# Router logits taken from the first normalised tile, and routing two blocks behind instead of three

## The reference

```python
x = x + xattn(layernorm(x), ctx, Wq, bq, Wk, bk, Wv, bv, Wo, bo)
h = layernorm(x)
expert = argmax(h @ router_w.T + router_b)
y = relu(relu(h @ weights1[expert] + bias1[expert]) @ weights2[expert] + bias2[expert])
x = x + y
```

## Time and profile before

| | us |
|---|---|
| median of 3 runs | 1223.89 (1223.77 to 1226.08) |
| the profiled execution, its own time | 1223.15 |
| its span in the profile | 1221.3 |
| PE busy | 1097.5 (90%) |
| DVE busy | 925.0 (76%) |
| ACT busy | 858.5 (70%) |
| POOL busy | 847.3 (69%) |
| mean granted TensorE clock | 0.972 of full |

### The profile page before, as it was taken

One profiled execution on the slowest core, in us unless ns is written; L12 is line 12 of the kernel. 1 busy time (PEld: TensorE's weight loads), 2 busy tenths in 40 slices (PEclk: granted clock), 3 DMA queues, 4 the chain that ended last, 5 costly groups with the idle time before them and its releaser, 6 DMA issues.

```text
span 1221.3 us, 39225 instructions
## 1 busy us (share of the span) xinstructions
PE 1097.5 (90%) x15399; PEld 845.1 (69%) x15399; DVE 925.0 (76%) x2321; ACT 858.5 (70%) x2020; POOL 847.3 (69%) x1613
## 2 busy tenths in 40 slices
PE   5999999999999999999999999999998419998893
PEld 4777777777777777777777777777776319977772
DVE  4787888888888888888888888888877427866772
ACT  4777777777777777777777777777776306655551
POOL 4544777677777777777777777777764656777776
PEclk9999999999999999999999999999999859999997
DMA  7415222522222222222222222222110136676650
GB/s 243 147 56 121 71 72 71 142 80 76 76 73 79 82 83 75 80 71 72 72 78 74 72 71 72 71 72 72 59 41 29 52 132 205 198 215 205 205 161 17
DMA packets 91156, 120.40 MB, mean 99 GB/s; under 512 B 14096, under 2 KB 73883, under 8 KB 90781
## 3 DMA queue, kind: packets, MB, share of 16 engines
q1 hardware_dynamic: 77150, 84.04, 24.2%
q0 software_dynamic: 13824, 33.85, 7.7%
HBM read 60.61 MB, written 59.31 MB: 98 GB/s over the span
## 4 chain that ended last, share of the span: by engine, by line
PE 60%; DVE 20%; POOL 7%; DMA 5%; issue 4%; ACT 3%; SPq 1%; POOLq 0%; DVEq 0%; ACTq 0%
PE pB L832 10%; PE pA L774 9%; PE pB L824 8%; PE sc L782 7%; DVE mx L595 6%; PE sc L806 5%; POOL out L419 4%; PE sc L765 4%; PE sc L815 3%; ACT arena L468 3%; DVE nrm L621 3%; PE m L791 3%; PE sc L1000 3%; DMA out<-arena 2%; PE m L798 2%
## 5 line engine op out<-in xcount | busy, mean ns | idle before, releaser
L595 DVE TENSOR_REDUCE mx<-m 128x4 bf16<-128x512 f32 x512 | 322.6, 670 | 10.7 <-PE m L791 10.5
L468 ACT ACTIVATE arena<-sc 128x512 f32<-128x512 f32 x512 | 264.5, 603 | 47.5 <-PE sc L815 47.5
L419 POOL DMA_INDIRECT out<-arena x160 | 157.0, 981 | 60.9 <-issue 31.1
L615 DVE STREAM_TRANSPOSE tr<-pB 128x512 f32<-128x512 f32 x128 | 91.8, 717 | 106.3 <-PE pB L824 106.3
L806 PE MATMUL sc<-qk 32*128 32x256 f32 x2048 | 167.0, 397 | 0.5 <-DVE rbp L674 0.5
L824 PE MATMUL pB<-arena 128*32 128x128 f32 x4096 | 159.8, 276 | 1.5 <-issue 1.0
L386 POOL DMA_INDIRECT pages<-row,slot_i x128 | 130.4, 1019 | 40.0 <-issue 37.0
L832 PE MATMUL pB<-wo_s,aT 128*128 128x256 f32 x512 | 138.0, 392 | 8.7 <-DVE aT L626 8.7
L824 PEld LDWEIGHTS pB<-arena 128*32 128x32 f32 x4096 | 99.0, 109 | 44.6 <-issue 43.6
L774 PE MATMUL pA<-cHi,wqkv 128*128 128x512 f32 x252 | 119.0, 474 | 9.4 <-DVE wqkv L660 9.4
L774 PE MATMUL pA<-xnT,wqkv 128*128 128x512 f32 x372 | 124.7, 443 | 0.0
(11 more groups left out here) (141 smaller groups left out, 2714.9 us busy)
## 6 DMA issues: line engine op xcount, KB each, us to landing
arena<-pages SPq DMA_DIRECT2D x160, 130.0 KB
cT<-ctxT SPq DMA_DIRECT2D x64, 256.0 KB, 3.8
xs<-x_in SPq DMA_DIRECT2D x128, 128.0 KB, 3.3
pages<-empty SPq DMA_DIRECT2D x120, 130.0 KB, 3.1
pages<-empty SPq DMA_DIRECT2D x1, 5200.0 KB, 19.8
out<-arena POOLq DMA_INDIRECT x160
w2s<-w SPq DMA_DIRECT2D x1, 2080.0 KB
qk<-w SPq DMA_DIRECT2D x1, 2064.0 KB, 8.2
```

Source lines behind the costliest of these rows:

```text
L419: pool.indirect_dma_start(out_rows, bass.IndirectOffsetOnAxis(pr[:, r, COL_TOKEN:COL_TOKEN + 1].bitcast(U32), 0), pr[:, r, 0:D], None, bou ...
L468: act.activation(pt[:, u % 2, g].rearrange("p i k -> p (i k)"), sc[g][:, :], ACT.Exp).then_inc(S["exp_out"], 1)
L595: ins = dve.tensor_reduce(mx[:, 32 * g:32 * g + 4], mb[i][:, :].rearrange("p (h k) -> p h k", h=4), AX.X, ALU.max)
L615: dve.transpose(tr[:, :], pB[:, :]).then_inc(S["tr_out"], 1)
```

## The change

The centred router weights are multiplied into the output projection: `wo_s` and `bo_s` get 32 more columns, and so do `xs` and `row`. The part of the logits that comes from x itself is made from the first normalised tile: its transposed float32 copy `xnTf` goes through `logits` and `logits_transpose` a block ahead, in u=1, and VectorE (`x_logits`) multiplies with the deviation `sd1` and puts it into the 32 columns of `xs`. `residual` then adds both parts. `best` multiplies with the second norm's reciprocal deviation and adds the router's bias. `xn2`, its transposes and copies go. `xnT` and its low half are made from `xnTf` in SBUF. Routing runs one block earlier, `rstd2` once a block, `rstd1` a block earlier, `slot_sum`, `choose`, `scan` and some `stats1` stand ahead of `attended`. Setup makes the combined weights and biases. On SP the wait on `scattered` goes and the context loads move. The columns of `row` get another order.

```diff
-COL_TOKEN, COL_EXPERT, COL_MEAN, COL_RSTD = 256, 257, 258, 259
+COL_TOKEN, COL_EXPERT, COL_MEAN, COL_RSTD, X0 = 0, 1, 2, 3, 4
...
-            load_ctx(3, 0)
-            load_ctx(3, 1)
...
                     after(sp, "x2_out", 4, q, u)
-                    if u == 3 and q >= 2:
-                        after(sp, "scattered", 64, q - 2, 63)
                     if live(q + 4):
                         load_x(q + 4, u)
                     n = FIRST_PAGES + 4 * q + u
                     if n < PAGES:
                         sp.dma_start(page_view[:, n, :], empty[:, :]).then_inc(S[f"fill{q % 4}"], 16)
-                    if u == 3 and live(q + 4):
-                        load_ctx(q + 4, 0)
-                    if u == 0 and q >= 1 and live(q + 3):
-                        load_ctx(q + 3, 1)
+                    if u in (1, 2) and live(q + 3):
+                        load_ctx(q + 3, u - 1)
...
-                r, m, g = rs1[:, q % 2, :], nm1[:, q % 2, :], ag1[:, q % 2]
+                r, m, v, g = rs1[:, q % 2, :], nm1[:, q % 2, :], vr1[:, q % 2, :], ag1[:, q % 2]
                 after(pool, "agg1_out", 4, q, 3)
                 if q >= 2:
                     after(pool, "xn_out", 2, q - 2, 1)
-                pool.tensor_scalar(r, g[:, :, 1], EPS, None, ALU.add).then_inc(S["var1_out"], 1)
+                    after(pool, "lg_out", 1, q - 2, 0)
+                pool.tensor_scalar(v, g[:, :, 1], EPS, None, ALU.add).then_inc(S["var1_out"], 1)
                 after(pool, "var1_out", 1, q, 0)
-                pool.tensor_tensor(r, r, half[:, :], ALU.pow).then_inc(S["pow1_out"], 1)
+                pool.tensor_tensor(r, v, half[:, :], ALU.pow).then_inc(S["pow1_out"], 1)
                 after(pool, "pow1_out", 1, q, 0)
                 pool.tensor_tensor(m, g[:, :, 0], r, ALU.mult).then_inc(S["mr1_out"], 1)
+                pool.tensor_tensor(sd1[:, q % 2, :], v, r, ALU.mult).then_inc(S["std1_out"], 1)
                 after(pool, "mr1_out", 1, q, 0)
                 pool.tensor_scalar(m, m, -1.0, None, ALU.mult).then_inc(S["rstd1_out"], 1)
 
-            def rstd2(q, h):
-                r, m = row[:, q % 4, 2 * h:2 * h + 2, COL_RSTD], row[:, q % 4, 2 * h:2 * h + 2, COL_MEAN]
-                after(pool, "sq_out", 4, q, 2 * h + 1)
+            def rstd2(q):
+                r, m = row[:, q % 4, :, COL_RSTD], row[:, q % 4, :, COL_MEAN]
+                after(pool, "sq_out", 4, q, 3)
                 pool.tensor_scalar(m, m, -1.0 / D, None, ALU.mult).then_inc(S["mean2_out"], 1)
                 pool.tensor_scalar(r, r, EPS, None, ALU.add).then_inc(S["eps2_out"], 1)
...
+                    pool.wait_ge(S["bo_out"], 2)
                 after(pool, "xn_out", 2, q, 1)
-                pool.tensor_tensor(xs[:, q % 4], xs[:, q % 4], bo_s[:, :].unsqueeze(1).to_broadcast([P, QB, D]),
+                after(pool, "lg_out", 1, q, 0)
+                pool.tensor_tensor(xs[:, q % 4], xs[:, q % 4], bo_s[:, :].unsqueeze(1).to_broadcast([P, QB, D + E]),
                                    ALU.add).then_inc(S["xb_out"], 1)
...
             rstd1(0)
             split(1)
-            for s in range(-1, NQ + 3):
+            rstd1(1)
+            for s in range(-1, NQ + 2):
+                if live(s - 2):
+                    slots_as_integers(s - 2)
+                    scatter(s - 2)
                 if live(s - 1):
-                    rstd2(s - 1, 0)
-                if live(s - 3):
-                    place(s - 3)
-                if live(s + 2):
-                    rstd1(s + 2)
+                    rstd2(s - 1)
                 if s >= 0 and live(s + 2):
                     split(s + 2)
-                if live(s - 3):
-                    slots_as_integers(s - 3)
                 if live(s + 1):
                     add_bo(s + 1)
-                if live(s - 3):
-                    if live(s - 1):
-                        after(pool, "sq_out", 4, s - 1, 3)
-                    scatter(s - 3)
                 if live(s - 1):
-                    rstd2(s - 1, 1)
-                if live(s - 2):
-                    meta(s - 2)
-                    fresh_pages(s - 2)
+                    meta(s - 1)
+                if live(s + 3):
+                    rstd1(s + 3)
+                if live(s - 1):
+                    fresh_pages(s - 1)
+                    place(s - 1)
...
             def xnT_copy(q, h):
+                at = slice(2 * P * h, 2 * P * (h + 1))
                 after(act, "xnT_done", 2, q, h)
-                act.activation(xnT[:, 0, :, 2 * P * h:2 * P * (h + 1)], xnT_bank(q, h)[:, :].rearrange("p (c t) -> p c t", c=2),
-                               ACT.Copy).then_inc(S["xnT_out"], 1)
-
-            def xn2T_copy(q, h):
-                after(act, "xn2T_done", 2, q, h)
-                act.activation(xn2T[:, :, 2 * P * h:2 * P * (h + 1)], xn2T_bank(h)[:, :].rearrange("p (c t) -> p c t", c=2),
-                               ACT.Copy).then_inc(S["xn2T_out"], 1)
+                if q >= 1:
+                    after(act, "xnTl_out", 2, q - 1, h)
+                act.activation(xnTf[:, :, at], xnT_bank(q, h)[:, :].rearrange("p (c t) -> p c t", c=2), ACT.Copy).then_inc(S["xnTf_out"], 1)
+                after(act, "xnTf_out", 2, q, h)
+                act.activation(xnT[:, 0, :, at], xnTf[:, :, at], ACT.Copy).then_inc(S["xnT_out"], 1)
 
...
+                    if s == -1 and u == 2:
+                        logits_copy(0)
+                    if u == 2 and live(s - 1):
+                        rank_copy(s - 1)
                     if s == -2 and u == 2:
                         for v in range(QB):
                             norm1(0, v)
                     if s >= 0 and live(s + 2):
                         for v in normal_rows(s, u):
                             norm1(s + 2, v)
-                    if u in (0, 2) and live(s - 1):
-                        norm2(s - 1, u)
-                        norm2(s - 1, u + 1)
...
-                dve.scalar_tensor_tensor(row[:, q % 4, u, 0:D], pB[:, 0:D], 1.0, xs[:, q % 4, u, :], ALU.mult, ALU.add,
+                dve.scalar_tensor_tensor(row[:, q % 4, u, X0:X0 + D + E], pB[:, 0:D + E], 1.0, xs[:, q % 4, u, :], ALU.mult, ALU.add,
                                          accum_out=row[:, q % 4, u, COL_MEAN:COL_MEAN + 1]).then_inc(S["x2_out"], 1)
 
             def xnT_lo(q, h):
                 after(dve, "xnT_out", 2, q, h)
                 hi, lo = (xnT[:, n, :, 2 * P * h:2 * P * (h + 1)] for n in range(2))
-                dve.tensor_tensor(lo, xnT_bank(q, h)[:, :].rearrange("p (c t) -> p c t", c=2), hi.bitcast(F32),
+                dve.tensor_tensor(lo, xnTf[:, :, 2 * P * h:2 * P * (h + 1)], hi.bitcast(F32),
...
+            def x_logits(q):
+                after(dve, "lgT_done", 1, q, 0)
+                after(dve, "std1_out", 1, q, 0)
+                if q >= 4:
+                    after(dve, "x2_out", 4, q - 4, 3)
+                dve.tensor_tensor(xs[:, q % 4, :, D:D + E], sc[3][:, 0:P].rearrange("p (u e) -> p u e", e=E),
+                                  sd1[:, q % 2, :].unsqueeze(2).to_broadcast([P, QB, E]), ALU.mult).then_inc(S["lg_out"], 1)
+
             def best(q):
-                after(dve, "lg_out", 1, q, 0)
+                after(dve, "rstd2_out", 1, q, 0)
+                if q >= 1:
+                    after(dve, "eq_out", 1, q - 1, 0)
+                own("scaled_out", q + 1, dve.tensor_tensor(lg[:, :, :], row[:, q % 4, :, X0 + D:X0 + D + E],
+                                                           row[:, q % 4, :, COL_RSTD].unsqueeze(2).to_broadcast([P, QB, E]), ALU.mult))
+                own("z_out", q + 1, dve.tensor_tensor(lg[:, :, :], lg[:, :, :], rb_s[:, :].unsqueeze(1).to_broadcast([P, QB, E]), ALU.add))
                 own("top_out", q + 1, dve.tensor_reduce(top[:, :], lg[:, :, :], AX.X, ALU.max))
...
+            def centre_router():
+                dve.wait_ge(S["setup_products"], 2)
+                own("wr_centred", 1, dve.tensor_tensor(wr_s[:, :, :], wr_s[:, :, :], sc[0][:, 0:E].unsqueeze(1).to_broadcast([P, 2, E]), ALU.subtract))
+                own("wr_centred", 2, dve.tensor_reduce(shift_e[:, :], wr_s[:, :, :], AX.X, ALU.add))
+                own("wr_centred", 3, dve.tensor_scalar(shift_e[:, :], shift_e[:, :], 1.0 / E, None, ALU.mult))
+                dve.tensor_tensor(wr_s[:, :, :], wr_s[:, :, :], shift_e[:, :].unsqueeze(2).to_broadcast([P, 2, E]), ALU.subtract).then_inc(S["wr_centred"], 1)
+                dve.tensor_copy(bvT[:, :, :].rearrange("p c t -> p (c t)"), sc[0][:, P:3 * P]).then_inc(S["setup_copies"], 1)
 
...
                         maxima(s, u, 1)
+                    if u == 0 and live(s - 2):
+                        slot_sum(s - 2)
+                    if u == 2 and live(s - 1):
+                        choose(s - 1)
+                    if u == 3 and live(s - 1):
+                        scan(s - 1)
+                    if u < 2 and live(s + 3):
+                        stats1(s + 3, (u,))
```

(126 more changed lines are left out.)

155 lines of the change are left out of this document (70 added, 85 removed).

## The result

The changed kernel takes 1326.45 us (median of 4 runs, 1323.28 to 1327.92), the kernel before 1224.93 beside it (4 runs, 1223.77 to 1226.08): a ratio of 1.0825, 95% interval 1.0799 to 1.0852, slower. Forecast were 1312 and a range of 1200 to 1350. The profiled execution has a span of 1323.2 us, 101.9 more than before. The last residual starts at 1082.07 for 964.79, +117.3; the last scatter lands 19.7 us behind it (1099.32 + 2.46 - 1082.07) for 34.7, -15.0; the phase over the pages is as long as before within 0.4 us. The loss sits in the main loop.

The account below looks back on a forecast made before the run. TensorE was taken to set the pace: a block of 27.9 + 0.4 + 0.93 + 3.0 = 32.2 us, 28 times +81. Clock +14, setup +3, block 1 +5, tail -14.5 gave +88.5: 1312 us, range 1200 to 1350.

Parts of the forecast that it names:

- TensorE's floor: Main-loop block of four batches: transposes and two waits go, output projection gets wider, leaving 27.9 us for 29.30.
- late copies: u=0 and u=1: `xnT_lo` waits for ScalarE's second copy, delaying `residual`, maxima and `max_transpose`; 0.4 us a block.
- undisturbed `best`: Step u=2: with no collision, TensorE would wait 0.47 us for the maxima, less than the old 0.70.
- `best` meets `add_bo`: Step u=2: GpSimd's `add_bo` holds `scaled` or `z` on VectorE, so TensorE waits 3.0 us a block for the maxima.
- The scan waits for GpSimd: Step u=3: VectorE's `scan` waits for `fresh_out`, behind `rstd1` on GpSimd, delaying the projection; 0.93 us a block.
- The clock: Main loop: TensorE's clock may fall after the 3 us pause, costing nothing or 1.6 us a block; 0.5 taken.
- rival 3: Main loop: the clock falls in every block, 45 us for 14, so 1343 us; chance 0.17.
- the tail: End of routing: from last residual to last scatter landed 20.2 us for 34.7, 14.5 less.
- Block 1: Block 1 gets a `best`, a scan wait and ranks that it lacked: 5 us (3 to 7).
- The first scores: Setup: products, first logits and copies stand ahead of them in TensorE's queue: 3 us later (1 to 5).
- rival 1: Step u=2: `best` and `add_bo` miss one another or operands aren't held; block 29.7, total 1225 us; chance 0.14.
- Rival 2: `fresh_out` precedes the scan's need, `add_bo` follows `best`: block 28.4, total 1188 us; chance 0.22 including faster mixtures.

Follow-up runs that it names:

- e6: e3 with GpSimd's `add_bo` held until VectorE's `nrm` of the step u=2 has ended: 1202.68 us, ratio 0.9822 to the kernel before.
- e9: e7 with GpSimd's `cLo` held until VectorE's `eq` has ended: 1186.81 us, ratio 0.9697 to the kernel before.
- after: The changed kernel as first measured, without any follow-up edit: 1326.45 us, ratio 1.0825 to the kernel before.
- e1: The changed kernel with `add_bo` moved behind `meta` in GpSimd's queue: 1274.55 us, ratio 1.0404 to the kernel before.
- e4: The changed kernel with z, the product that adds the router's bias in `best`, left out: 1315.3 us, ratio 1.0756 to the kernel before.
- e7: e6 with the scaling and the bias of the router's scores moved to GpSimd, right behind `rstd2`: 1201.74 us, ratio 0.9807 to the kernel before.
- e5: The kernel before with its scatter moved ahead of `add_bo` in GpSimd's queue: 1327.92 us, ratio 1.0847 to the unedited kernel before.
- e2: The changed kernel with `fresh_pages` moved ahead of `rstd1` in GpSimd's queue: 1297.34 us, ratio 1.061 to the kernel before.
- e3: The changed kernel with both moves, `add_bo` behind `meta` and `fresh_pages` ahead of `rstd1`: 1237.04 us, ratio 1.01 to the kernel before.

## Why the prediction was right

**TensorE's floor** was 27.9 us a block, 0.4 for late copies beside it, 0.47 for an undisturbed `best`: 28.77 with no collision. e6 has 28.79. The sum is right, its parts less so, and that they add up is partly luck. No run shows the 0.4: `max_transpose` of u=0 and u=1 doesn't wait, and u=0 takes 6.68 us for a forecast of 6.95 that had 0.25 of lateness in it. Instead the floor is nearer 28.1 (e9, where TensorE waits for no maxima, has 28.28 with 0.17 of waiting), and an undisturbed `best` costs 0.55 to 0.70 in e6. In the kernel before VectorE had 17% of the block to spare, a little more than the sixth that the prediction allows it.

**`best` meets `add_bo`:** 3.0 us forecast, 2.86 measured in the block shown. Its price above the undisturbed wait is 2.31, the step u=2 at full clock in after less that in e6 (10.07 - 7.75), for a forecast of 2.53. The place was right too: z is held, `scaled` slips in ahead. e1 and e6 move `add_bo` away and the wait falls to 0.56; e4 shows that it isn't z as such. The Trainium skill, "SBUF — State Buffer", section "Who interferes with whom", gives this as a lock between the two engines for two SBUF operands; the 2.31 against 0.29 us of z, with no other edit than GpSimd's order between them, agrees, and so do `nrm` in e1, `eq` in e4 and e7 and `pick` in e9. `hot` in e5 is held as well, but by the records it had started first, while in that section whoever comes first goes first. That `mx`, which reads PSUM and no SBUF, ran its usual 1.29 us beside `cLo` in e9 agrees as well.

**The scan waits for GpSimd:** 0.93 forecast; TensorE's wait is 1.10, and without it a block is 1.37 to 1.39 shorter at full clock (e2, and e3 against e1). `fresh` and `tr` moved as described: `fresh` is there 3.97 us into u=3 for 3.9, `tr` starts at 4.39 for 4.2. This term was taken too small by 0.4 us.

**The clock** is the other: 0.5 us forecast as a hedge between 0 and 1.6, 0.79 measured (33.07 - 32.28). It doesn't fall in every block, as rival 3 had it, but in two of three, and such a block is for the most part 1.0 us longer, not 1.6. With the others the block came out at 33.07 for 32.7; over 28 blocks that is 10 of the 14 us that were missed.

**The ends:** the tail 19.7 us for 20.2. Block 1 takes 33.20 us (60.32 to 93.52) for 26.80 before: 6.4 more, for a forecast of 5. The first scores start 5.3 us later than before (33.93 for 28.66), for a forecast of 3; which of the setup's products took more than I counted was not tried.

**The rivals:** rival 1 (they miss one another) is out by z's 2.60. Rival 2 (neither wait, 1188) isn't this kernel, but reordering comes near it: 1202.68 in e6, and 1186.81 in e9, which has two operations on GpSimd besides. Its 1188 assumed a block of 28.4; e9 has 28.28.

**Of the experiments' forecasts,** those of e1 and e3 (1230, and 1195 to 1200, for 1274.55 and 1237.04) failed at one step: I took a GpSimd operation out of one VectorE operation's way without asking which one it would meet next. e7's (1193, for 1201.74) failed in the same way. e5's was too small, as `hot` was held before `add_bo` even showed.

That the clock falls behind the pause and not for another reason rests on e1, e3 and e6, where the pause is 0.54 to 0.72 and the granted clock 1.00 in every block between 140 and 840 us, and on e2, where the pause is as before and the clock still falls. Why it stays up in a third of after's blocks, whose pause is as long, is open.

## What to carry to other kernels

When two engines can hold one another, list for each long GpSimd operation what VectorE does in its 2 to 3 us, before and after an edit; a move that frees one victim often finds the next, and the cheapest cure here was a wait that starts the long operation right behind the short one. Read the changed kernel's mean by line against the same operation's undisturbed duration: 2311 ns for 292 names the fault at once. Take the order apart before judging a change: here one kernel 8% slower and one 3% faster than the old differ in GpSimd's order, two waits and the engine of two small operations.

## What the runs showed of the hardware that was not expected

- How small the margin is. By the records `scaled` starts at 504.08, `add_bo` at 504.32 and z at 504.54. `scaled` waits for the end of `cLo` (504.36), is done at 504.51, and costs `add_bo` at most 0.02 us (2.67 for the 2.65 of e6); z, due 0.03 behind `scaled`, stands until 507.14. From 107 to 1001 us this is so in every block, within some hundredths: `scaled` ends 0.15 behind `cLo` and takes 0.41 to 0.58 for 0.29.
- In e5 `hot` started at 525.87 by its record, `add_bo` at 526.38, and yet `hot` ended at 528.89, behind `add_bo` (528.74). The same offset of 0.50 us is there in the blocks at 559.79 and 592.27. Before `add_bo` GpSimd issued its last scatter (525.30 to 526.36). In the kernel before, a `hot` beside a scatter's issue took 0.29 us. Whether GpSimd holds the way already while it still issues, or the records are off, no run here decides.
- The same pause doesn't always cost the clock. In the changed kernel, between 140 and 840 us, all 21 blocks have a pause of 2.85 to 3.02 us; 13 have a mean granted clock of 0.95, one has 0.90 and 7 have 1.00. In e5, with 3.42 in all of them, 0.95, 0.95 and 0.90 follow one another from 262 us on (the block with the 7.6 us at 0.57 is one of the last kind). Where TensorE waits 0.54 to 0.72 us for the maxima (e1, e3, e6) it was 1.00 throughout.
